# Down weights of a mixture of experts loaded expert by expert, with two more turned experts and written-out engine lists

## What is computed

```python
g = jnp.einsum('bsh,ehf->ebsf', x, w_gate)
u = jnp.einsum('bsh,ehf->ebsf', x, w_up)
h = jax.nn.silu(g) * u
expert_out = jnp.einsum('ebsf,efh->ebsh', h, w_down)
cw = router_probs * gate_weights
cw = cw / (jnp.sum(cw, axis=-1, keepdims=True) + 1e-09)
out = jnp.einsum('ebsh,bse->bsh', expert_out, cw)
```

## Time and profile before

| | |
|---|---|
| median of 3 runs | 816.68 us (816.19 to 817.64) |
| span of the profiled execution | 814.5 us |
| the profiled execution's own time | not listed beside its span |
| TensorE, VectorE, ScalarE, GpSimd busy | 96%, 75%, 48%, 45% |
| mean granted TensorE clock | 0.996 |
| moved by DMA | 48.59 MB |

### The profile page before, as it was taken

The page is one execution under the profiler, slowest core; times in us unless marked ns, Lnnn a source line. Parts: engine busy times, 40 slices in busy tenths (PEclk is TensorE's granted clock), DMA queues, the critical chain, the costliest instruction groups (busy, mean ns, idle before and its releaser), DMA issues. The chain is left out here.

```text
span 814.5 us, 13287 instructions
## 1 busy us (share of the span) xinstructions
PE 781.0 (96%) x4637; PEld 658.8 (81%) x4637; DVE 611.2 (75%) x1270; ACT 391.9 (48%) x798; POOL 365.2 (45%) x304
## 2 busy tenths in 40 slices
PE   8999999999998998997999999998999999999997
PEld 5988787888877887786788788887888788877886
DVE  6673775589859895577989989887677678856773
ACT  5353336534485353564243675234333455457552
POOL 4564012077713964622644865955335224421123
PEclk9999999999999999999999999999999999999999
DMA  9500000011000142123321020142124303000110
GB/s 295 133 12 1 1 2 1 1 52 53 27 27 27 71 116 89 38 65 118 104 78 52 27 78 27 53 129 79 52 74 137 115 14 114 4 1 13 54 39 14
DMA packets 29531, 48.59 MB, mean 60 GB/s; under 512 B 7777, under 2 KB 14601, under 8 KB 29465
## 3 DMA queue, kind: packets, MB, share of 16 engines
q1 hardware_dynamic: 28744, 47.47, 18.6%
q10 hardware_dynamic: 720, 0.27, 0.1%
HBM read 33.02 MB, written 14.71 MB: 59 GB/s over the span
## 5 line engine op out<-in xcount | busy, mean ns | idle before, releaser
L1837 PEld LDWEIGHTS bank<-w_down,sh_buf 128*128 128x128 f32 x1664 | 220.9, 192 | 34.8 <-DVE sh_buf L2481 13.4
L1837 PE MATMUL bank<-w_down,sh_buf 128*128 128x128 f32 x1664 | 230.2, 277 | 9.3 <-DVE sh_buf L2481 9.1
L1565 ACT ACTIVATE sh_buf<-bank 128x512 f32<-128x512 f32 x256 | 151.0, 595 | 183.0 <-PE bank L1837 111.8
L2481 DVE TENSOR_TENSOR sh_buf<-sh_buf,bank 128x512 f32<-128x512 f32 x248 | 167.2, 682 | 79.7 <-PE bank L1837 58.8
L1837 PE MATMUL bank<-z_hi,w_lo 128*128 128x512 f32 x512 | 224.4, 438 | 0.0
L1837 PE MATMUL bank<-z_hi,w_hi 128*128 128x512 f32 x512 | 202.3, 395 | 0.0
L1837 PE MATMUL bank<-z_lo,w_hi 128*128 128x512 f32 x512 | 202.1, 395 | 0.0
L1837 PEld LDWEIGHTS bank<-z_lo,w_hi 128*128 128x128 f32 x512 | 96.3, 188 | 22.4
L1837 PEld LDWEIGHTS bank<-z_hi,w_lo 128*128 128x128 f32 x512 | 97.5, 190 | 14.1 <-issue 2.2
L1837 PEld LDWEIGHTS bank<-z_hi,w_hi 128*128 128x128 f32 x512 | 97.4, 190 | 11.7 <-issue 0.5
L1360 POOL TENSOR_TENSOR backs<-backs,w_a 128x1024 f32<-128x1024 f32 x16 | 45.2, 2832 | 48.8 <-ACT w_a L1648 27.6
(11 more groups left out here) (274 smaller groups left out, 1217.4 us busy)
## 6 DMA issues: line engine op xcount, KB each, us to landing
trans_spill<-state SPq DMA_DIRECT2D x16, 512.0 KB, 2.6
backs<-chain_spill SPq DMA_DIRECT2D x16, 512.0 KB, 4.9
backs<-trans_spill SPq DMA_DIRECT2D x16, 512.0 KB, 3.3
backs<-keep_spill SPq DMA_DIRECT2D x4, 1024.0 KB, 5.5
cw_wide<-cw_spill SPq DMA_DIRECT2D x12, 256.0 KB, 3.3
x<-in_x SPq DMA_DIRECT2D x8, 128.0 KB, 3.9
backs<-in_w_gate SPq DMA_DIRECT2D x4, 256.0 KB, 5.7
backs<-in_w_up SPq DMA_DIRECT2D x4, 256.0 KB, 5.9
```

The source lines that it names most:

```text
L1565: act.activation(s_buf[:, m % 2, :], bank_of("gate", m)[:], ACT.Silu).then_inc(S["silu_done"], 1)
L1837: return pe.matmul(dst, lhs, rhs, start=start, stop=stop, **kw)
L2481: dve.tensor_tensor(h_buf[:, m % 4, :], s_buf[:, m % 2, :], bank_of("up", m)[:], ALU.mult).then_inc(S["h_done"], 1)
```

## The change

- `w_down` goes. `down_stage` has two places of 256 KB, and an expert's down weights are loaded from DRAM into one of them in every pass (for normal experts, and for all eight in the first pass).
- In the first pass each expert's weights are split (`down_hi` on ScalarE, `down_lo` on GpSimd or, new, VectorE, four each) into one of two slabs; each slab is spilled to DRAM, and loaded again (512 KB) for the turned experts of the last passes.
- Two experts of the first pass, 3 and 6, are turned: 14 in all.
- `RING` is 2, and the spread router weights have a ring of 2 of their own; they are made by one transpose of 32 rows and not by four, and laid out differently in DRAM.
- `y_weighted` is the memory of `turned_part`, with waits that keep the two apart.
- Loads of raw gate and up weights from the third expert on share a semaphore in pairs.
- The planner is replaced by written-out lists (`ITEMS`, `SEQUENCE`, `HOMES`), and the flags differ: `Y1S` gives block 2's second sum to VectorE (TensorE's list has 8 `y1` for 12, VectorE's 8 for 4), `HIDES` 8 experts for 2, `ADDS` 25 of the experts' adds to VectorE for 32 and 25 to GpSimd for 20, `LOWS` 36 rests to VectorE for 40 and 20 to GpSimd for 8. The link products stay on their engines.

The core of the diff:

```diff
-DOWNS = [0, 0, 0, 0, 0, 0, 0, 0, ...
+DOWNS = [0, 0, 0, 1, 0, 0, 1, 0, ...
-RING = 3
+RING = 2
+CW_RING = 2
+STAGES = 2
+SLABS = 2
-Y1S = [1, 1, 1, 0]
+Y1S = [1, 1, 0, 0]
...
-        w_down = sb("w_down", P, E, FC, C)
+        down_stage = sb("down_stage", P, STAGES, FC, C)
+        slab = sb("slab", P, SLABS, 2, FC, C, dtype=F32R)
...
-        y_weighted = sb("y_weighted", P, BT)
+        y_weighted = turned_part
...
+            def load_stage(e):
+                n = staged_before(e)
+                if n >= STAGES:
+                    older = stages[n - STAGES]
+                    if older < E:
+                        sp.wait_ge(S["down_split"], older + 1)
+                    if not DOWNS[older]:
+                        sp.wait_ge(S["y_full"], older + 1)
+                sp.dma_start(down_stage[:, n % STAGES], a["w_down"][e % E].rearrange("(f p) h -> p f h", p=P)).then_inc(stage_in[n % STAGES], 16)
+
+            def spill_slab(e):
+                sp.wait_ge(S["down_split"], e + 1)
+                sp.dma_start(slab_spill[e], slab[:, e % SLABS].bitcast(F32)).then_inc(slab_out[e % SLABS], 16)
+
+            def load_slab(e):
+                s = slabs.index(e) % SLABS
+                for i in range(SLABS):
+                    sp.wait_ge(slab_out[i], 16 * (E // SLABS))
+                older = slabs[slabs.index(e) - SLABS]
+                if DOWNS[older]:
+                    sp.wait_ge(S["y_full"], older + 1)
+                sp.dma_start(slab[:, s].bitcast(F32), slab_spill[e % E]).then_inc(slab_in[s], 16)
...
-            sp.dma_start(w_down[:], a["w_down"].rearrange("e (f p) h -> p e f h", p=P)).then_inc(S["w_in_d"], 16)
+            for e in range(STAGES):
+                load_stage(e)
...
+                    act.wait_ge(S["turn_summed"], summed(eg))
...
             def down_high(i):
-                if i == 0:
-                    act.wait_ge(S["fin_rdy"], 2 * UNITS)
-                    act.wait_ge(S["kept_a"], 32 * BLOCKS)
-                    act.wait_ge(S["kept_b"], 32 * BLOCKS)
-                    act.wait_ge(S["spilled"], 16 * L)
+                stage_filled(act, i)
+                if i >= SLABS:
+                    act.wait_ge(slab_out[i % SLABS], 16 * (i // SLABS))
+                    if DOWNS[i - SLABS]:
+                        act.wait_ge(S["y_full"], i - SLABS + 1)
...
-                for i in range(G):
-                    ins = pe.transpose(bank_named[name][0:E, i * P:(i + 1) * P], cw[:, q % 2, i, :], ident[:])
-                ins.then_inc(S["cw_turned"], 1)
+                pe.transpose(bank_named[name][0:G * E, 0:P], cw[:, q % 2].rearrange("p g e -> p (g e)"), ident[:]).then_inc(S["cw_turned"], 1)
```

More of the change, by code:

```diff
@@ L25 @@
 AHEAD_W = 6
-LAG = 2
 E, F = 8, 512
@@ L613, in slowed @@
-def slowed(busy, now):
-    if now < WARM:
-        return 0.0
-    share = 0.0
-    for back in (0.4, 1.3, 2.1, 3.0):
-        last = now - back
-        first = last - 3.41
-        work = 0.0
-        for a, b, w in reversed(busy):
-            if b <= first:
-                break
-            if a < last and b > a:
-                work += w * (min(b, last) - max(a, first)) / (b - a)
-        if work < 1700:
-            share += 0.23
-    return share
-WORK = dict(gate=1536, up=1536, down=512, T2=1024, W2_part=1024, W2=128, T2_back=128, read=1024, read_back=512, y0=1024, y1=1024, y1_back=512, y0_back=128, front_hidden=930, tokA=1350, link=32, starts=1200, finish_T=512,
-            back_hidden=1224, back_out=2048, tokB=1024, route=128, kv=2048, r=1024, mid_out=1024, lend=0, lend_w=0, lend_log=0)
@@ L825, in every @@
-def every():
-    ops = experts() + weights() + attn_a()
-    for u in range(UNITS):
-        ops += chain(u)
-    for j in range(BLOCKS):
-        ops += front(j) + steps(j) + back(j)
-    for q in range(BLOCKS):
-        ops += middle(q)
-    for q in range(PASSES):
-        ops += ffn_input(q)
-    ops += [pe(("biases",), 1.25, on("pe", "gate", 24), takes=((("biases",), on("dve", "biases")),)), dve(("biases",), 4.4, on("pe", "biases")),
-            dve(("restart", 0), 1.75, on("dve", "mix", 3))]
-    ops += [sp(("store", j), 4.0, pass_end(BLOCKS + j)) for j in range(BLOCKS)]
-    return ops
@@ new lines, in orders @@
+def orders():
+    out = {}
+    for engine, text in SEQUENCE.items():
+        items = {kind: iter(args) for kind, args in ITEMS[engine].items()}
+        out[engine] = []
+        for word in text.split():
+            kind, _, times = word.partition("*")
+            for _ in range(int(times or 1)):
+                out[engine].append((kind,) + next(items[kind]))
+    return out
+ORDER = orders()
+BANKS = "01234567"
+BANK = {(kind,) + arg: home for kind, (args, homes) in HOMES.items() for arg, home in zip(args, homes)}
@@ L1073, in build, with staged_before, stage_filled, slab_filled @@
         turned = turned_chunks()
+        def staged_before(e):
+            return stages.index(e)
+        def stage_filled(engine, e):
+            n = staged_before(e)
+            engine.wait_ge(stage_in[n % STAGES], 16 * (n // STAGES + 1))
+        def slab_filled(engine, e):
+            s = slabs.index(e) % SLABS
+            engine.wait_ge(slab_in[s], 16 * sum(slabs.index(i) % SLABS == s for i in slabs if E <= i <= e))
         def written(*write):
@@ L1097, in summed, with added_by_pool @@
             return sum(DOWNS[i] and not is_first(i) for i in range(e))
+        def added_by_pool(e):
+            return max([written("pool", ("add", i)) for i in range(e) if not ADDS[i] and not DOWNS[i]], default=0)
         def turned_passes(q):
@@ L1971, in down @@
                     return
+                if f == 0 and half == 0:
+                    stage_filled(pe, e)
                 pe.wait_ge(S["h_done"], m + 1)
```

1077 lines of the change are left out of this document (482 added, 595 removed), and 49 rows, old and new, of tables (ITEMS, SEQUENCE).

## The result

The changed kernel takes 806.12 us (median of 4 runs, 805.14 to 807.27) against 817.16 for the kernel before on the same chip (816.19 to 817.81): a ratio of 0.9871 [0.9856, 0.9887], 11.0 us less. Forecast were 4.0 us less. The profiled execution took 805.14 us with a span of 803.3, 11.2 less than the span before. So the direction and the range held, and the size did not: the gain is nearly three times the forecast. The time is near that of the rival *The new list also closes other gaps* (806.7, given 0.13).

What follows compares the result with a forecast made beforehand. TensorE, busy 781.0 of 814.5 us, was taken as the bound, with the second chain setting its stretch's end. Outside +3.0 (-1.6 + 4.6), inside -7.0, together -4.0; plus 2.2 from span to time: 812.7 us, range 805 to 820.5.

Steps and rivals of the forecast that it cites:

- The new list also closes other gaps: Rival, faster still: half of the gaps like the 4.48 us at the first chain's end close, another 6 us: 806.7; chance 0.13.
- Part 1, two more turned experts: First pass, experts 3 and 6: TensorE loses 1.6 us of work, counted in full because TensorE sets the pace there.
- Part 2, Y1S: Block 2's second product, 616 to 646 us: TensorE -4.0 us, VectorE +4.9 us, where TensorE isn't what ends.
- the chain term: Second unit's end to block 2's norm: 7 of 12.3 us surplus go, ends nothing (0.8 us slower) or 12.
- Part 3, the split: Split leaves second chain: the 3.19 us stand goes, some 3 us return after sixteen links; no TensorE gain booked.
- Part 4, the chain: Second unit's end to block 2's norm: 107.9 us falls 7.0 to 100.9; two chunks moving out add 4.6 us outside.
- The signs that the prediction named for being right: 64 fewer 128-column down records, block 2's transposes gone, no block of eight subtractions, second chain's stretch near 101 us.
- those for being wrong: TensorE waiting for a down_stage or slab load, a stand over 4 us after sixteen first links, the stretch still at 108.
- Part 5, edits at nothing: New loads and spills on SP's queue, products moved to GpSimd, new waits, smaller rings: all costed at nothing.
- Streamed weights come late: Rival, slower: loads on SP's in-order queue come late at four places, 3 us each, +12: 824.7 us; chance 0.10.
- GpSimd's new work slows each chunk: Rival, slower: 47 us more GpSimd work adds half a microsecond to 24 chunks, +12: 824.7 us; chance 0.08.
- The chain hardly shortens: Rival, same time: second chain loses 3 us instead of 7, cancelling against the moved chunks: 816.7; chance 0.15.

## Why the prediction was right or wrong

**Part 1, two more turned experts: wrong.** The work was sized rightly (1.5 us, of which 1.45 show), the step that failed is "It counts in full, because the first pass is a stage in which TensorE sets the pace". What I left out is the engines that take over: 8 rests, 8 copies and the sums beside the linear recurrence, which cost 2.43 us at once. To `up` 72 TensorE's work falls by 2.3 us and the stage gets 2.0 longer; the two experts are about 1 us of that, and what makes the rest was not tried.

**Part 2, Y1S: the work was right, its place wrong.** "This lies in 616 to 646, where TensorE isn't what ends" let the -4.0 vanish in the chain term. In the new list the sums in TensorE's queue cost 5.4 us (at the places that I gave them; others were not tried). The argument read the stretch of the kernel before and held it to be the same in the new list. My reading, argued and not shown by a run, is that TensorE is further ahead there and its transposes stand directly between the read-back and the norm. In the old list the argument holds more than I had it: there the edit loses 2 us.

**Part 3, the split: right in what it saw, without the gain it seemed to bring.** The block is gone, and 2.13 us of standing came back at the sixteen first links, for the 3 forecast. The reading of the 10.16 us block was incomplete: it has the silu behind ScalarE's copies, but not that the copies wait for a store. Without the subtractions beside them TensorE still stood for 3.66 us, and with the copies moved too for 1.62.

**Part 4, the chain: the stretch nearly right, its worth not.** The stretch is 102.5 us (528.50 to 630.98) for 100.9 forecast, and TensorE is busy for 91.55 us of it, for 93.2 forecast. Two and a half chunks moved out for the two forecast (+5.7 us for +4.6). By itself the term gives -5.4 + 5.7, about nothing, and not the gain of 2.4. What the forecast missed here are two products held by GpSimd, worth 2 to 3 us. The signs that the prediction named for being right all came (64 records fewer, no block, a stretch near 101 us), and none of those for being wrong: they tested the parts that cancel, and not the two steps that made the gain.

**Part 5, edits at nothing: right for the loads, wrong for the order.** Outside the chain's stretch 706.6 us became 700.8, 5.8 less, for 3.0 more in the forecast. The wrong step is the sentence against the last rival, "around the first chain both lists have the same products (chunks 83 to 105) and links". That compared products and links, and not the other tasks between them: `restart` had moved sixteen links, away from a wait for a store, and the prediction has no term for it. It carries 3.7 us in the new list, and with the 5.4 of Y1S the whole gain: with both undone nothing is left that can be measured. The stand of 4.48 us became 0.82 in the new list whether `restart` was early or late; that comes with the lists as a whole, and which tasks carry it was not settled.

**The rivals.** *Streamed weights come late*: not seen; no wait of TensorE for a load, and a `slab` load takes 3.5 us at the median. *GpSimd's new work slows each chunk*: the lengthening is there, but the last stage, where most of that work lies, is 4.0 us shorter all the same. VectorE's rests take 950 ns each for 709 before, its expert products, with one operand in PSUM, 680 for 682. This is what the prediction drew from the Trainium skill (GPSIMD Engine Reference, Specifications): the trace agrees that the rests, with two SBUF inputs, suffer, and the products with a PSUM input don't. *The chain hardly shortens*: it shortened by 5.4 us, and the reason for no gain did not come true. *Other gaps*: the outcome in part, at 0.13 too low, since the argument against it was a comparison half made. That its 806.7 is met is luck: it comes from halving the gaps, and about half of the gain is Y1S, which is none of them.

## What to carry to other kernels

Where engines work through written-out lists, compare the two lists task by task, the small ones too, and ask of every task what store or load must have landed before it may run: a memset that waits for a store held 60 links and TensorE behind them. The price of an edit belongs to the list around it: the same two edits were worth 3.7 and 5.4 us in one order, some 1.4 and -2 in the other, so an edit's share in a large change is found by undoing it in the kernel after. Price work that leaves the bounding engine twice, once as hidden and once in full, and widen the range by the difference.

## What the runs showed of the hardware that was not expected

**VectorE can stand still for as long as a GpSimd instruction runs.** A product of 1024 elements with two operands in SBUF takes 1.22 us alone. In the kernel after it takes 3.44 and 3.42 us (602.64, 614.34) when GpSimd starts a product at the same moment:

```profile
602.61 2.38 POOL L1232 TENSOR_TENSOR backs<-backs,w_a 128x1024 f32<-128x1024 f32 x1 [6.04 <-DVE w_a L2675]
608.48 2.38 POOL L1232 TENSOR_TENSOR backs<-backs,w_a 128x1024 f32<-128x1024 f32 x1 [3.49 <-DVE w_a L2675]
614.31 2.36 POOL L1232 TENSOR_TENSOR backs<-backs,w_a 128x1024 f32<-128x1024 f32 x1 [3.46 <-DVE w_a L2675]
```

The excess of 2.2 us is nearly the whole of GpSimd's instruction, 2.38. The reduction at 609.04, with one input and under the second of these, takes 1.21, as ever. So the price depends on which instruction of VectorE runs beside GpSimd's, and an edit of the order can take it away.

**A stand of TensorE can cost more than its length.** The granted clock falls to 0.50, which is 1.2 of 2.4 GHz, behind some stands. Stretches of the kernel before, behind the stand of 4.48 and that of 3.19 us:

```profile
370.80:374.10 3.30, 3.25 (x30) 3.26 (x32) 2.99 (x5) 1.19 (x2) 0.00 (x0) 0.50 0.68 233
562.00:565.20 3.20, 3.19 (x12) 2.66 (x11) 2.65 (x7) 0.86 (x2) 3.20 (x3) 0.50 0.02 5
```

and of the kernel after, behind 0.82, 2.13 and 2.98 us:

```profile
367.80:371.20 3.40, 3.40 (x38) 3.06 (x39) 3.40 (x6) 1.58 (x3) 0.00 (x0) 1.00 0.61 205
552.20:555.40 3.20, 3.20 (x12) 2.91 (x13) 2.54 (x8) 1.25 (x3) 1.35 (x3) 0.50 0.58 164
618.40:621.80 3.40, 3.39 (x20) 3.00 (x21) 3.37 (x4) 1.20 (x2) 2.24 (x1) 1.00 0.00 0
```

Behind the 2.13 us the clock fell and behind the 2.98 it did not, so the length of the stand alone does not decide it. Nor does the program: in another execution of the same kernel it fell behind this stand as well:

```profile
619.27 1.01 PE L1710 MATMUL bank<-down_stage,sh_buf 128*128 128x128 f32 x3 [2.96 <-DVE sh_buf L2355]
...
619.20:622.60 3.40, 3.33 (x12) 3.05 (x13) 3.37 (x5) 0.60 (x1) 2.18 (x1) 0.51 0.00 0
```

There chunk 180's `up`, ahead of the stand, starts 0.87 us later than in the execution above, and chunk 181's, behind it, 2.39. So the lower clock cost 1.5 us, and part of the spread between executions of one kernel comes from it. With the late `restart` in the kernel before, the granted clock from 360 to 445 us was 0.94 on average, for 0.98 without it, and there, in that one execution, the 2.3 us that the edit had gained by 368.55 were lost again.
